# A hand-written order of four tiles for every engine of a six-layer windowed attention block

## The reference

```
x = attn(layernorm_modulated(x)); x = mod * x         # part a: 16 heads of 8, causal, softmax
for layer in 6:                                        # part b
    qkv = x_shifted @ Wqkv[layer]                      # 128 -> 3 x 1024, 16 heads of 64
    q, k = l2norm(q) * qs, l2norm(k) * ks              # then rotary tables
    sim = 8 * q @ k.T   over windows of 32 and the window before;  a = softmax(sim)
    x = x + (a @ v) @ Wo[layer]                        # 1024 -> 128
    h = layernorm(x_shifted) * g + b
    x = x + (h @ W1a * gelu(h @ W1g)) @ W2 + b2        # 128 -> 341 -> 128
out = x0 + mod5 * x                                    # part c
```

## Time and profile before

| | us |
|---|---|
| median of 3 runs | 3695.43 (3693.75 to 3704.42) |
| span of the profiled execution | 3699.1 |
| PE busy | 3521.4 (95%) |
| DVE busy | 3039.5 (82%) |
| ACT busy | 2586.6 (70%) |
| POOL busy | 2309.1 (62%) |

### The profile page before, as it was taken

The page is one execution under the profiler, slowest core; times in us unless marked ns, Lnnn a source line. Parts: engine busy times, 40 slices in busy tenths (PEclk is TensorE's granted clock), DMA queues, the critical chain, the costliest instruction groups (busy, mean ns, idle before and its releaser), DMA issues. The chain is left out here.

```text
span 3699.1 us, 146879 instructions
## 1 busy us (share of the span) xinstructions
PE 3521.4 (95%) x63940; PEld 2694.0 (73%) x63940; DVE 3039.5 (82%) x4947; ACT 2586.6 (70%) x4028; POOL 2309.1 (62%) x1364
## 2 busy tenths in 40 slices
PE   6999996999999999999999999999999999999996
PEld 4777774777777777777777777777777777777774
DVE  5767766988889988888888888888898888888883
ACT  3565554677777777777777777777777777777773
POOL 1110104767777777777777767777777777776761
PEclk9999998999999999999999999999999999999998
DMA  2000001212222222222222222222222222222212
GB/s 75 4 4 7 4 7 43 56 48 58 56 58 63 64 56 58 56 56 62 58 56 58 54 56 64 56 58 55 64 63 58 56 57 54 56 56 54 54 49 68
DMA packets 121989, 188.76 MB, mean 51 GB/s; under 512 B 24942, under 2 KB 43142, under 8 KB 120972
## 3 DMA queue, kind: packets, MB, share of 16 engines
q1 hardware_dynamic: 121356, 179.36, 18.7%
HBM read 24.08 MB, written 4.19 MB: 8 GB/s over the span
## 5 line engine op out<-in xcount | busy, mean ns | idle before, releaser
L1325 POOL TENSOR_TENSOR rc<-rc,rs 128x1024 f32<-128x1024 f32 x384 | 912.9, 2377 | 349.2 <-DVE rs L1391 348.5
L1331 POOL TENSOR_TENSOR rc<-rc,rnorm 128x1024 f32<-128x1024 f32 x384 | 723.7, 1906 | 392.9 <-DVE rnorm L162 331.4
L1385 DVE TENSOR_TENSOR rc<-proj,rope_b 128x1024 f32<-128x1024 f32 x384 | 466.7, 1215 | 96.1 <-ACT squares L1177 89.6
L1177 ACT ACTIVATE squares<-proj 128x1024 f32<-128x1024 f32 x384 | 394.0, 1026 | 151.1 <-PE proj L921 137.6
L1013 PEld LDWEIGHTS ring<-pT,vmoved 64*64 64x64 f32 x18432 | 381.2, 135 | 132.8 <-issue 132.8
L1391 DVE TENSOR_TENSOR rs<-proj,rope_b 128x1024 f32<-128x1024 f32 x384 | 466.2, 1214 | 0.0
L958 PEld LDWEIGHTS ring<-ident,rc 128*128 128x128 f32 x3072 | 364.2, 142 | 137.5 <-issue 52.2
L1399 DVE TENSOR_REDUCE sums<-squares 128x16 f32<-128x1024 f32 x384 | 455.3, 1186 | 1.1 <-issue 0.9
L1013 PE MATMUL ring<-pT,vmoved 64*64 64x32 f32 x18432 | 407.7, 220 | 37.9 <-issue 36.4
L958 PE MATMUL ring<-ident,rc 128*128 128x128 f32 x3072 | 426.3, 277 | 11.6 <-POOL rc L1331 6.6
L1013 PE MATMUL ring<-pT,vown 64*64 64x32 f32 x6144 | 381.9, 219 | 13.8 <-issue 13.8
(11 more groups left out here) (176 smaller groups left out, 7886.1 us busy)
## 6 DMA issues: line engine op xcount, KB each, us to landing
vmoved<-vown SPq DMA_DIRECT2D x576, 128.0 KB
vmoved<-vown SPq DMA_DIRECT2D x192, 192.0 KB
vmoved<-vown SPq DMA_DIRECT2D x576, 64.0 KB
wqkv_raw<-in_L_ffn_Wqkv SPq DMA_DIRECT2D x40, 192.0 KB, 2.7
wo<-in_L_ffn_Wo SPq DMA_DIRECT2D x6, 512.0 KB, 4.2
x_attended<-xtok SPq DMA_DIRECT2D x8, 256.0 KB, 2.0
xtok_c<-x_attended SPq DMA_DIRECT2D x8, 256.0 KB, 4.2
out<-xtok_c SPq DMA_DIRECT2D x8, 256.0 KB, 2.4
```

What stands on the lines that cost most here:

```text
L1177: nc.scalar.activation(squares[:, c, :], proj[c][:, :], ACT.Square).then_inc(sq_done, 1)
L1325: nc.gpsimd.tensor_tensor(rc[:, k % 2, c, :], rc[:, k % 2, c, :], rs[:, c, :], ALU.add).then_inc(add_done, 1)
L1331: nc.gpsimd.tensor_tensor(dst, dst, rnorm[:, k % 2, c * HEADS:(c + 1) * HEADS].rearrange("p (h o) -> p h o", o=1).broadcast_to([P, HEADS, ...
L1385: nc.vector.tensor_tensor(rc[:, k % 2, c, :].rearrange("p (h d) -> p h d", h=HEADS), proj[c][:, :].rearrange("p (h d) -> p h d", h=HEADS), ...
```

## The change

The loop over steps becomes a loop over rounds, `for n in ROUNDS`, one round a sequence, and on each engine the round is a list in which each of the four tiles has its own order. `ring_order` follows PE's list. So that the lists may differ in order between q and k, the counting semaphores `proj_full`, `sq_done`, `ss_done`, `turned_done`, `add_done` and `unit_done` become pairs, one for each c, and each helper states all its waits itself (`turned`, `after`). POOL gets `norms_pass(k)`, which does no work: it only waits until DVE's chain of norms of tile k is done. No instruction that computes is added or taken away; PE gets 709 more instructions that only wait (4536 for 3827). The core of the diff:

```diff
-LAST_STEP = NT + 6
+ROUNDS = range(-1, NSEQ + 2)
...
+            def norms_pass(k):
+                if tile(k):
+                    pool.wait_ge(rn_done, (min(k, NT) + 1) * RSQRT_STEPS)
...
+            for n in ROUNDS:                      # on PE
+                values(4 * n + 1, 1)
...
+                mean(n - 1)
+                weigh(4 * n)
...
+                variance(n - 1)
+                transpose_qk(4 * n + 2, 1)
+                project(1, 4 * n + 4)
+                transpose_qk(4 * n + 2, 2)
+                transpose_qk(4 * n + 2, 0)
...
+                project(0, 4 * n + 4)
+                values(4 * n + 2, 0)
+                transpose_qk(4 * n + 2, 3)
+                score(4 * n + 2, 0)
+                transpose_probs(4 * n + 1, 0)
+                transpose_probs(4 * n + 1, 1)
+                score(4 * n + 2, 1)
+                weigh(4 * n + 1)
...
+                values(4 * n + 3, 0)
+                values(4 * n + 3, 1)
+                score(4 * n + 3, 0)
+                score(4 * n + 3, 1)
+                transpose_probs(4 * n + 2, 0)
+                transpose_probs(4 * n + 2, 1)
...
+                feed_up(n - 1, 0)
+                weigh(4 * n + 2)
...
+                feed_up(n - 1, 4)
...
+                values(4 * n + 4, 0)
+                score(4 * n + 4, 0)
+                score(4 * n + 4, 1)
+                transpose_probs(4 * n + 3, 1)
...
+                project(1, 4 * n + 6)
+                weigh(4 * n + 3)
...
+                project(1, 4 * n + 7)
+                score(4 * n + 5, 0)
+                score(4 * n + 5, 1)
+                transpose_probs(4 * n + 4, 0)
...
+            for n in ROUNDS:                      # on DVE
+                sums_of(4 * n)
+                norms_of(4 * n + 2)
+                turns_of(0, 4 * n + 3)
+                maxima(4 * n + 1)
+                square_sums(1, 4 * n + 3)
+                square_sums(0, 4 * n + 3)
+                less_maxima(4 * n + 1)
+                centre(n - 1)
+                turns_of(1, 4 * n + 3)
+                norms_of(4 * n + 3)
+                sums_of(4 * n + 1)
...
+            for n in ROUNDS:                      # on POOL
+                scale_probs(4 * n - 2)
+                norms_pass(4 * n)
+                make_rope(1, n)
+                scale_heads(0, 4 * n)
+                add_halves(1, 4 * n)
...
+                norms_pass(4 * n + 3)
+                scale_probs(4 * n + 1)
+                add_halves(1, 4 * n + 3)
```

More of the change, by code:

```diff
@@ L950, in transpose_qk @@
             def transpose_qk(k, i):
+                if not tile(k):
+                    return
                 half, c = divmod(i, 2)
-                if half == 0:
-                    pe.wait_ge(unit_done, 2 * k + c + 1)
+                pe.wait_ge(unit_done[c], k + 1)
                 bank = begin(f"T{i}", k)
@@ L967, in score @@
             def score(k, half):
+                if not tile(k):
+                    return
                 j = k % TILES
-                pe.wait_ge(ring_free, RING[f"T{2 * half + 1}", k] + 1)
-                if half == 0:
-                    need(pe, scr_masked, k)
+                if half == 0 and k == 0:
+                    mask_first_scores()
+                pe.wait_ge(ring_free, max(RING[f"T{2 * half}", k], RING[f"T{2 * half + 1}", k]) + 1)
+                need(pe, scr_masked, k)
                 pe.sem_inc(pe_passed, 1)
@@ L994, in transpose_probs, with weigh @@
                 last.then_inc(ring_full, 1)
[L996 to L1002, removed]
+            def weigh(k):
+                if not tile(k):
+                    return
+                begin("O0", k)
+                begin("O1", k)
+                pe.wait_ge(ring_free, max(RING["P0", k], RING["P1", k]) + 1)
+                pe.wait_ge(moved, (k + 1) * 7 * 16)
                 banks = [ring_bank(f"O{i}", k)[:, :].rearrange("p (q k) -> p q k", q=PAIRS) for i in range(2)]
@@ L1005, in weigh @@
                 last = [None, None]
-                for p in range(4 * half, 4 * half + 4):
+                for p in range(PAIRS):
                     for odd in range(2):
@@ L1016, in weigh, with output @@
                                     start=True, stop=True)
[L1017 to L1021, removed]
+                for i in range(2):
+                    last[i].then_inc(ring_full, 1)
+            def output(n, half):
+                if not seq(n):
+                    return
                 pe.wait_ge(wo_in, 16 * (n // BATCH + 1))
                 pe.wait_ge(ring_free, RING["O1", TILES * n + 2 * half + 1] + 1)
-                proj_emptied(0, g + 1)
                 bank = proj_bank(0, 1 - half)
@@ L1185, in values_out @@
             def values_out(k, b):
+                if not tile(k):
+                    return
+                if k > 1:
+                    act.wait_ge(ring_full, RING["O1", k - 2] + 1)
                 if b == 0:
@@ L1200, in widen_deviation, with squared_deviation @@
+            def squared_deviation(n):
+                if not seq(n):
+                    return
+                act.wait_ge(centred, n + 1)
+                need(act, down_full, n)
+                nc.scalar.activation(xq, xc[:, :], ACT.Square).then_inc(xq_done, 1)
+            def widen_deviation(n):
+                if not seq(n):
+                    return
+                k = TILES * (n + 1) + 3
                 act.wait_ge(rn_done, (min(k, NT) + 1) * RSQRT_STEPS)
+                need(act, down_full, n)
@@ L1311, in make_rope @@
             def make_rope(half, n):
+                if not starts_layer(n):
+                    return
                 tiles = slice(2 * half, 2 * half + 2)
-                need(pool, turned_done, n * 8 - 4 + 4 * half)
+                for c in range(2):
+                    need(pool, turned_done[c], TILES * n - 2 + 2 * half)
                 pool.wait_ge(qks_in, 32 * (n // BATCH + 1))
@@ L1408, in norms_of @@
                 if tile(k):
[L1409 removed]
+                    for c in range(2):
+                        dve.wait_ge(ss_done[c], k + 1)
                     ss = sums[:, 0:2 * HEADS]
```

666 lines of the change are left out of this document (386 added, 280 removed).

## The result

The changed kernel took 3862.48 us (median of 4 runs, 3852.84 to 3864.75) against 3694.65 us for the kernel before (4 runs, 3693.75 to 3704.42): a ratio of 1.0453, with a 95% interval of 1.043 to 1.0475. It is slower by 4.5%. The forecast of 3729 us had the sign right and the size wrong, and the time lies outside the range (3640 to 3785).

A forecast was written before the change was run, and what follows sets the result against it. PE was taken to bound the kernel, idling when instructions ran out. Terms of -1.4, +1.9 and +0.2 us gave +0.7 a sequence, +34 us over 48, so 3729 us, 0.9% slower; 8-in-10 range 3640 to 3785.

The forecast's parts named there:

- What bounds the kernel: PE sets the pace; its idle time, 2.0 us a sequence, is running out of fetched instructions in weighs and scores.
- Changes between small and large matmuls: On PE, fewer visits to small matmuls and no projection straight after them: -1.4 us a sequence, bounds -1.8 and -0.9.
- Running out of instructions: PE's holes in weighs and whole scores grow from 2.0 to 3.9 us a sequence: +1.9, bounds -2.0 and +2.7.
- 51/165: Holes total 51 us over 165 weighs; three weighs behind large matmuls kept that rate, 0.31 us each, 0.9 together.
- Waits of PE for others: PE's waits on other engines in the tighter order, such as POOL's scaling: +0.2 us a sequence, bounds 0 and 1.0.
- POOL's place: norms_pass keeps POOL waiting for DVE's chain of norms, as before; worth 0 on PE, covered by DVE's idle time.
- The sum: The terms -1.4, +1.9 and +0.2 give +0.7 us a sequence, +34 us over 48.
- holes don't grow: Rival: PE's holes depend on where packets fall, not stretch length; 3637 us, faster; chance 0.27 with half growth included.
- POOL's place makes PE wait: Rival: late norms of tile 4n+3 delay POOL's scaling and the weigh of 4n+1; 3796 us, slower; chance 0.12.
- The forecast of what the profile would show: Per sequence PE busy about 59.5 us, idle about 4; holes late in whole scores and early in tile 4n+1's weigh.

The follow-up runs named there:

- fixed packets: 2560 PE instructions a sequence, empty ones setting where packets end: kernel before 0.9783, 1.0259 or 0.9759 by place; changed kernel 0.9794 or 1.0538.
- packets out of the way: Both kernels at 2560 PE instructions a sequence: kernel before with feed_down 60 into a packet, 3611.69 us; changed kernel with it 20 in, 3626.97 us.
- fixed at 75: Kernel before at 2560 PE instructions a sequence, feed_down 75 into a packet: 3622.9 us; the same with each score's halves joined: 3713.69 us.

## Why the prediction was wrong

*What bounds the kernel* was right: PE, and its idle time is the fetch of instructions. The runs with fixed packets show it more sharply than the forecast claimed it.

*Changes between small and large matmuls*, forecast -1.4 us a sequence with bounds -1.8 and -0.9. Measured: -0.7 (busy time less the part of the clock), -0.8 between the two kernels with packets out of the way. The direction holds, the size is half. Joining four pairs of halves took 0.55 us out of the scores themselves (6.30 to 5.75 us in one sequence), 0.14 each, where the sum had 0.22 and 0.11 for a projection behind. PE's busy time as a whole did not fall with it (61.52 us for 61.20, both fixed at 75), so this pair shows the saving inside the scores alone.

*Running out of instructions*, forecast +1.9, bounds -2.0 and +2.7. The idle time by "issue" rose from 1.38 to 3.54 us a sequence, +2.2 (all such waits of PE over the 43 periods). As idle time this was near, in part by luck, for two errors offset each other: scores got 1.07 us for the forecast 1.8, and weighs 2.75 for 1.9. The weigh behind half a score got 1.12 for 1.0, but the three that the forecast left at 51/165 got 1.64 for 0.9.

Here is the step that failed: the term priced a hole at its own length. About half of the holes of 1.2 us and more (193 of 397 below) were followed by half clock, and by the fits that cost 1.57 us a sequence. The kernel before gave a hint that I did not follow: it has 13.7 us at half clock itself. Over nine kernels (before, after and seven of the experiments; the others have three such falls of the clock in all), from 900 to 3500 us, the clock fell in or soon behind idle times of PE as often as this:

```
length of the idle time, us   0.4-0.6   0.6-1.2   1.2-1.5   1.5-1.8   over 1.8
idle times                      122       403       165       149        83
followed by half clock            0        20        51        83        59
```

and it fell behind nothing else. So the loss is not linear in the holes: in weighs 84 for 45, of 1.38 us for 1.14 each, came with twelve times the half clock.

*Waits of PE for others*, forecast +0.2, bounds 0 and 1.0. Waits for other engines rose from 0.04 to 0.32 us a sequence. Right, and `transpose_probs` waits for POOL by less than 0.1 us.

*POOL's place*, forecast 0. It was measured at -49 us in the changed kernel and -67 us with fixed packets. The reasoning "DVE has 6 us of idle time a sequence" failed: DVE's idle time lies elsewhere: of a hold of 1.6 us PE pays 1.3, so this chain has 0.3 us to spare. The step also took the 387 ns of the earlier trace rows as the size of a hold. In the kernel before these are ends of POOL's instructions, 0.3 us each in 101 of 158 chains; a hold lasts for what is left of POOL's instruction, and the scaling that starts just ahead of L152 has all of its 1.9 us left. And the step compared with the kernel before, not with the new order without the place.

*The sum*: -0.7 + 2.2 + 0.3 + 1.6 = +3.4 for +0.7. The difference of 2.7 is 1.6 of clock, 0.7 of changes, 0.3 of fetch and 0.1 of waits. Of the rivals, "holes don't grow" fails by the counts and "POOL's place makes PE wait" by the waits; its sign was the wrong one.

The forecast of what the profile would show was half right: idle time "about 4" came (3.94), PE's busy time of 59.5 did not (62.35), and the holes came early in the weigh of tile 4n+1.

## What to carry to other kernels

Before reordering a kernel whose engine is full and issues in short bursts, find out where its packets of instructions end: with a whole number of packets a period and one shift, the kernel before gained 2.4% without a change in what it does, where the two orders in their best places lie 0.4% apart. Price a hole of TensorE by what the clock does behind it, not by its length alone, and look at single sequences, since a mean over slices hides it. When VectorE runs a chain of tiny instructions on data in SBUF, keep GpSimd from starting a long one beside it; one wait at the right place does it.

## What the runs showed that I had not expected

Empty instructions can be worth 174 us (the kernel before) or 278 us (after), by where they put the ends of packets. The order of the change, in the better place tried for it, is nearly even with the old one: 3627 against 3612 us (ratios 0.9794 and 0.9759). The Trainium skill, "Runtime: NRT & Kernel Launch", section "Instruction fetch mechanics", has the fetch hidden by the pace of issue; these runs contradict it for PE, whose holes end 2.5 us after the next packet began to move. Half clock costs 0.45 us per us in nearly every kernel that has enough of it. What stays open is what makes a packet begin to move late, so also how much of the holes in weighs belongs to the cover ahead of each, and whether the new order without the hole in the weigh of tile 4n+1 would go below 3612 us; neither was tried.
